# A two-layer LoRA and expert kernel on one core: gates of the next batch's first tile brought forward on VectorE, three other steps moved behind

## What is computed

```
def layer0(x, lang):                          # x: [8, 256, 1024]
    c = x @ W0.T + 2 * lora(x, A0c, B0, gates) # gates: softmax over the top 2 of
                                               # x @ Wr0.T + 5 * one_hot(lang)
    r = c @ route_w.T                          # top 1 expert, weighted by its logit
    return x + expert(c, A0f, Bw, r)
def layer1(x, slot):
    c = x @ W1.T + b1 + 2 * (x @ lora_As[slot]) @ lora_Bs[slot]
    g = softmax over the top 2 of c @ W_router.T
    return x + c @ Wb.T + b_base + 2 * experts(c, A1, B1, g)
```

## Time and profile before

| what | value |
|---|---|
| median of 3 runs | 488.05 us (486.38 to 489.43) |
| the profiled execution | 491.27 us, of which the span is 489.2 us |
| PE busy | 473.4 us, 97% of the span |
| DVE busy | 326.8 us, 67% |
| ACT busy | 154.4 us, 32% |
| POOL busy | 76.6 us, 16% |
| chain that ended last | PE 74%, DVE 18%, DMA 3%, ACT 2% |

### The profile page before, as it was taken

How to read it: one execution, slowest core, us unless ns; L and a number is a source line. 1 busy time by engine, 2 the same in 40 slices (tenths; PEclk the granted TensorE clock), 3 DMA queues, 4 the chain that set the end, 5 groups by cost and what they waited for, 6 DMA issues and landing times.

```text
span 489.2 us, 8342 instructions
## 1 busy us (share of the span) xinstructions
PE 473.4 (97%) x2911; PEld 435.4 (89%) x2911; DVE 326.8 (67%) x955; ACT 154.4 (32%) x339; POOL 76.6 (16%) x66
## 2 busy tenths in 40 slices
PE   5999999999999999999999999999999999999997
PEld 4988998999998889988899999999999999999996
DVE  3566664567476969858857856865965965973842
ACT  4445531132222246213323423313323322321310
POOL 2031000000000241240240230221222222030010
PEclk9996999999999999999999999999999999999999
DMA  7985534821010301332421520430422322300202
GB/s 234 337 277 193 149 111 125 145 86 37 25 38 33 92 3 23 46 44 81 74 45 34 120 46 17 122 47 11 118 47 31 109 45 45 109 2 2 102 1 86
DMA packets 88417, 40.25 MB, mean 82 GB/s; under 512 B 68503, under 2 KB 82465, under 8 KB 88254
## 3 DMA queue, kind: packets, MB, share of 16 engines
q1 hardware_dynamic: 88110, 39.25, 30.7%
q0 software_dynamic: 272, 0.56, 0.5%
HBM read 28.64 MB, written 11.16 MB: 81 GB/s over the span
## 4 chain that ended last, share of the span: by engine, by line
PE 74%; DVE 18%; DMA 3%; ACT 2%; issue 2%; SPq 0%; DVEq 0%; ACTq 0%
PE banks L1384 22%; PE banks L1386 21%; PE banks L1385 21%; PE banks L1379 5%; DVE left L911 3%; DVE ybuf L1102 2%; DVE x_raw L959 2%; DMA x_raw<-in_L_cond_W_dram 2%; PE banks L1625 1%; PE banks L1433 1%; DVE b_acc L1199 1%; DVE G L911 1%; DVE x_raw L1071 1%; DMA fe_lo_dram<-fe_keep_lo 1%; ACT left L654 1%
## 5 line engine op out<-in xcount | busy, mean ns | idle before, releaser
L1384 PE MATMUL banks<-G,left 128*128 128x460 f32 x224 | 88.1, 393 | 0.0
L1385 PE MATMUL banks<-G,left 128*128 128x460 f32 x224 | 82.9, 370 | 0.0
L1386 PE MATMUL banks<-G,left 128*128 128x460 f32 x224 | 82.8, 370 | 0.0
L594 POOL TENSOR_TENSOR xTlo<-x_raw,xThi 128x512 fp32r<-128x512 f32 x28 | 41.0, 1487 | 264.4 <-ACT xThi L654 127.4
L1384 PE MATMUL banks<-WbThi,ws_hi 128*128 128x460 f32 (+1 forms) x216 | 75.2, 348 | 0.5 <-DVE Mdir L911 0.5
L1386 PE MATMUL banks<-WbThi,ws_lo 128*128 128x460 f32 (+1 forms) x216 | 73.3, 339 | 0.0
L1385 PE MATMUL banks<-WbTlo,ws_hi 128*128 128x460 f32 (+1 forms) x216 | 73.1, 338 | 0.0
L654 ACT ACTIVATE left<-x_raw 128x512 fp32r<-128x512 f32 x64 | 38.8, 628 | 64.1 <-DVE x_raw L1071 29.3
L1384 PEld LDWEIGHTS banks<-G,left 128*128 128x128 f32 x224 | 42.3, 189 | 4.7 <-DVE wzTlo L911 0.5
L1386 PEld LDWEIGHTS banks<-G,left 128*128 128x128 f32 x224 | 42.0, 188 | 4.7
L1385 PEld LDWEIGHTS banks<-G,left 128*128 128x128 f32 x224 | 42.3, 189 | 2.6
(11 more groups left out here) (211 smaller groups left out, 1020.9 us busy)
## 6 DMA issues: line engine op xcount, KB each, us to landing
x_raw<-in_x_dram SPq DMA_DIRECT2D x56, 128.0 KB, 3.6
out_dram<-ybuf SPq DMA_DIRECT2D x14, 512.0 KB, 3.0
x_raw<-in_L_cond_W_dram SPq DMA_DIRECT2D x10, 512.0 KB, 5.4
wraw<-in_L_cond_W_dram SPq DMA_DIRECT2D x6, 512.0 KB, 5.2
wraw<-in_L_ffn_W_base_dram SPq DMA_DIRECT2D x4, 512.0 KB, 6.2
x_raw<-in_L_ffn_W_base_dram SPq DMA_DIRECT2D x4, 512.0 KB, 5.7
xin_first<-in_x_dram SPq DMA_DIRECT2D x1, 1024.0 KB, 10.7
x1T_dram<-xin_first SPq DMA_DIRECT2D x1, 1024.0 KB, 4.2
```

Source lines behind the costliest of these rows:

```text
L594: return gp.tensor_tensor(out_, a, b, ALU.subtract)
L1384: pe.matmul(out_, l[0], r[0], start=start, stop=False, **kw)
L1385: pe.matmul(out_, l[0], r[1], start=False, stop=False, **kw)
L1386: return pe.matmul(out_, l[1], r[0], start=False, stop=stop, **kw)
```

## The change

On DVE, `gates0` of the next batch's first tile used to stand behind `y_c12` and `turn_x(1, ...)` of the slot that ends. Now it stands right behind the third sum, S2. `turn_x(1, ...)` comes behind the gates, in the next slot, then S2's remainder, and `y_c12` behind hgTlo of the first tile. S4's sum leaves the place behind hgTlo and stands behind `keep_p16`. On ACT, hgThi of the first tile now comes ahead of xThi of the second, and S4's rounding moves behind hgThi of the second tile. On PE, only slot 0 changes: one step of the Strassen products (step 44) is done ahead of the fourth ffn0 and not behind it. SP's and POOL's code is unchanged.

```diff
 # ACT, slot
                 if has_a:
+                    hgT_part(a)
                     xT_turned(a + 1, 1, x_raw[1 - turn])
-                    hgT_part(a)
                 s_part(b, turn, 2)
...
                 keep_p1(b)
-                s_part(b, turn, 3)
                 exp1(m + 1)
...
                     hgT_part(a + 1)
+                s_part(b, turn, 3)
                 if has_n:
                     xT_turned(n, 0, x_raw[turn])
 # DVE, slot
                 if has_a:
                     gates0(a, q, first_sums if b == 0 else None)
+                if 0 < b < NB - 1:
+                    dve.wait_ge(x_in[1], b * 64)
+                    turn_x(1, x_raw[1 - turn])
                 s_part(b, turn, 1)
                 hs_part(m, 0)
                 if has_a:
                     hgT_part(a)
-                s_sums(b, turn, (3,))
+                if b > 0:
+                    y_c12(b - 1)
                 hs_part(m + 1, 1)
...
                 keep_p16(b)
+                s_sums(b, turn, (3,))
                 if has_a:
                     hgT_part(a + 1)
                 keep_p15(b)
...
                     s_sums(q, 1 - turn, (2,))
-                y_c12(b)
-                if has_n:
-                    dve.wait_ge(x_in[1], b * 64 + 64)
-                    turn_x(1, x_raw[turn])
+                if b == NB - 1:
+                    y_c12(b)
 # PE, slot
-                        main_to((42, 43, 43, 44)[g] if first else (39, 40, 42, 43)[g])
+                        main_to((42, 43, 44, 44)[g] if first else (39, 40, 42, 43)[g])
```

## The result

| | before | after |
|---|---|---|
| median | 488.15 us (4 runs) | 520.16 us (4 runs, 518.62 to 523.17) |
| ratio | | 1.0666, 95% interval 1.0605 to 1.0727 |
| span of the profiled execution | 489.2 us | 521.1 us |

The kernel is 32 us slower; 17 were forecast, and the range ended at 513. The mechanism of the forecast is in the profile, and the price is nearly twice as large. Both profiled executions took some 3 us more than their medians (491.27 and 523.17 us), so their difference stands for that of the medians.

What follows compares the result with a forecast made beforehand. PE, busy 97%, was taken to bound the kernel. Terms 14.5 (slots 1 to 5) + 5.5 (slot 0) + 1.5 (clock) - 4.3 (gates) = +17.2 us on 488.05 gave 505.3 us, range 497 to 513.

Steps and rivals of the forecast that it cites:

- The mechanism of the forecast: S4's later sum delays the x load; DVE's turn of x comes 4.0 us late and PE waits for wzTlo.
- the forecast's steps: From DVE's turn of x to PE: to xThi 1.33, xThi and copy 1.2, to wzTlo 0.32, to PE 0.34 us.
- the gates' gain: At starts of slots 1 to 6, earlier gates end PE's wait for hg: 4.3 us gained, 1.45 of it at slot 1.
- what stands behind the gates: free: Steps now behind the gates cost nothing, hgTlo ready 0.2 us ahead; up to 0.5 us a slot without POOL's cover.
- Forecast 5.5 + 1.5 - 1.45: Slot 0: PE waits 5.5 us for the late x, 1.5 for a clock fall, less 1.45 gained at slot 1's start.
- the wait of 2.9 us in slots 1 to 5: PE waits for wzTlo: turn of x 4.0 us late, 1.1 swallowed by the chain; 14.5 us in all.
- nothing for waits of 2.9 (from 0 to 1.5 each): PE's clock in slots 1 to 5: no cost added behind these waits, at most 7.5 us in all.
- one row of a fallen clock and one wait of 1.3 us that left it: Clock evidence: 0.50 over 46 to 49 us, costing 1.5 us; 1.00 over 210 to 255 us despite waits for hg.
- Rival (c): PE's clock falls in most waits, or loads take 4 us to issue: +23 to +29, 511 to 517 us; chance 0.15.
- the hgTlo margin of 0.2 us: Behind the gates, hgTlo would be ready only 0.2 us ahead of add_lora0, costed at nothing.
- SP's wait for the S4 sum: Sign on SP's queue: the wait ahead of the x loads would grow by some 10 us a slot.
- The Trainium skill's fit: Rule against the loss: 512 KB loads in 3.2 us, not 6.2; sum near -2. The forecast rejected it from the trace.

Runs made afterwards that it cites:

- `s4_alone`: The kernel before the change with only S4's sum and its rounding moved to the later place; 523.17 us, ratio 1.0707.
- `turn_late`: The changed kernel with the new x's first-half turn (DVE) and high part (ACT) moved behind second-tile wzTlo and whTlo; 484.87 us, ratio 0.9913.
- `gates_alone`: The changed kernel with S4's sum and its rounding put back where they stood before the change; 488.28 us against 489.43, ratio 0.9975.

## Why the prediction was wrong

**Right: the mechanism and its place.** The S4 sum frees the buffer, the load lands 6.9 us later in slot 2 (6.2 were forecast), DVE's queue stands at the turn, ACT's at xThi, and PE at wzTlo behind step 36. `s4_alone` makes the loss alone, and `turn_late` takes it away with the load left late. From the turn's start to PE's resumption 3.17 us passed, 3.2 by the forecast's steps.

**Right: the gates' gain; wrong: "what stands behind the gates: free".** The wait for hg went. In `turn_late` a slot from the second on takes 37.93 us against 38.53, and the time ahead of slot 1's turn of hg shrank by 1.45, as forecast. But slots 0 and 1 lost 0.3 and 0.7 us ahead of their second turn of wz, the latter mostly in a wait of PE for hgTlo of 0.45, where the forecast had counted on 0.2 us of room; slots 0 to 5 together gain 3.5 us, not 4.3. That the kernel as a whole gains 0.87%, 4.2 us, is near the forecast partly by luck: its profile also has a higher clock ahead of the slots (0.93 against 0.80 over 35 to 60 us), which the change does not touch. The gain needs the S4 sum out of the way: `gates_alone` shows 0.25%.

**Right: slot 0.** Forecast 5.5 + 1.5 - 1.45 = +5.6, measured +5.2, with an idle time of 4.74 us and the clock fallen there as well.

**Mis-sized: the wait of 2.9 us in slots 1 to 5.** It measured 3.5 to 3.9, 18.5 us in place of 14.5. Two terms made it in slot 2. The sum began where it was forecast (284.96 in the old time) but took 1.55 us beside POOL, longer than any of the eight of the earlier trace rows; and the fourth block took 4.3 us to land, not 3.6.

**The step that failed: "nothing for waits of 2.9 (from 0 to 1.5 each)".** In the profiled execution the clock fell in all five slots, and a fall cost 2.4 us on average, more than the upper bound: 11.9 us of the 14.8 that were missing. I had one row of a fallen clock and one wait of 1.3 us that left it, and took the value of the shorter one for a wait of 2.9 and a fall of 3 us for the price. The row could not carry the price: it has no idle time at all (PE busy 3.00 of 3.00 us), and from 47.2 us on PE did products of 272 columns in it, not small turns. Nor would the forecast's own wait have been free: over all runs the clock fell behind 5 of the 9 idle times between 2.08 and 3.34 us, so that at 2.9 us an estimate is a fall in every second slot. Rival (c), falls in most waits, is what happened in the profiled execution, at 0.15; its 511 to 517 was still short by the longer wait (4.0 us) and by the price of a fall, 2.4 us and not 1.5.

**Also off:** in the changed kernel too the hgTlo margin of 0.2 us was not there in slot 1, where PE waited 0.49 for it; about 0.6 us in all. SP's wait for the S4 sum grew by 7.6 us a slot and not by 10, and slots 1 to 5 take 44.0 to 44.3 us and not 40.9. The Trainium skill's fit from "DMA: Bandwidth & Descriptors" ("Anatomy of one DMA"), given for the path of GpSimd, makes 2.3 us for a block of 128 KB by an estimate. It does not agree with these loads, which SP issues, here either: in slot 2 of the changed kernel they took 3.8 to 4.3 us a block.

## What to carry to other kernels

When a step is moved later, list who is released by it, the DMA queue too, and compare the move (11.1 us here) with the slack of the last of them (7.1), and then look at what stands in order behind that one: here it was enough to put the load's consumer behind two small pieces of work that PE waits for, which turned 6.7% slower into 0.9% faster. Price a wait of a busy PE twice, once for its length and once for the clock behind it, the second as a chance that grows with the wait times a price of its own (1.6 to 2.7 us here).

## What the runs showed of the hardware

- Idle times of PE that ended in wzTlo, over all runs and slots 0 to 5: behind the 9 of 3.37 us and more the granted clock was half each time, behind those of 3.21, 3.30 and 3.34 us once in three, between 2.08 and 2.58 us in 4 of 6, and behind the 7 from 1.10 to 1.93 us never.
- A fall cost 1.5 to 1.6 us in some slots (19.6 to 19.7 against 18.12, behind idle times of 2.1 to 3.6 us) and 2.3 to 2.7 in others (20.4 to 20.8 in the changed kernel, and the first two falls of `s4_alone`; behind 3.4 to 3.9). The windows of the changed kernel show the difference: the clock was low for a shorter time in slot 1 (mean 0.76, price 1.55) than in slots 2 to 5 (0.51 to 0.56).
- The sum over x_raw took 0.68 us alone and 1.28 beside a POOL subtraction before, and 1.55 where it began 0.3 us behind the start of one. In the changed kernel it ended 0.55 us behind POOL's subtraction each time (296.11 and 295.55 in slot 2). In `gates_alone`, where it began 0.17 us ahead of POOL (slot 2), it took 0.68, and POOL's two subtractions 2.91 and not 2.5. A conversion of 128x2 elements on DVE took 0.84 us there and 0.58 in `turn_late`, and not 0.17, and ended with POOL's work on xTlo (350.96 and 350.94; 348.59 and 348.56). It looks as if whichever starts later stands until the other is done. Which resource they share was not tried.
- The fourth block of 128 KB landed 3.6 us after its issue at one place of the slot and 4.3 at another; why was not tried.
